# Eight slots instead of four in the row-normalising stage of a graph network

## The reference

```python
h = jnp.maximum(_layernorm(x, axis=-1), 0.0)
x = x + _L0_gnn_ref(h, edge_index, edge_weight, ...)

def _bn(x, g, b):
    m = jnp.mean(x, axis=0)
    v = jnp.var(x, axis=0)
    return g * (x - m) * jax.lax.rsqrt(v + EPS) + b
```

## Time and profile before

| what | value |
|---|---|
| median of three runs | 4132.0 us |
| the profiled execution | 4137.27 us, span 4135.5 us |
| mean granted TensorE clock | 0.869 |
| TensorE, VectorE, ScalarE, GpSimd busy | 75%, 59%, 45%, 35% of the span |
| HBM traffic | 664 MB read, 528 MB written, 288 GB/s over the span |
| the normalising stage | first load 39 us, last GpSimd write issued by 665 us |

### The profile page before, as it was taken

One profiled execution on the slowest core, in us unless ns is written; L12 is line 12 of the kernel. 1 busy time (PEld: TensorE's weight loads), 2 busy tenths in 40 slices (PEclk: granted clock), 3 DMA queues, 4 the chain that ended last, 5 costly groups with the idle time before them and its releaser, 6 DMA issues. The chain is left out here.

```text
span 4135.5 us, 50004 instructions
## 1 busy us (share of the span) xinstructions
PE 3115.6 (75%) x11465; PEld 1891.5 (46%) x11465; DVE 2439.3 (59%) x5239; ACT 1850.5 (45%) x3090; POOL 1430.2 (35%) x1395
## 2 busy tenths in 40 slices
PE   2444443888888883999999999995999999844543
PEld 2444443444444441655655655553444444333432
DVE  4444443777777774888888888783444444433332
ACT  2544452666566661444444444442334444333332
POOL 0332334455555533333333333312222222024344
PEclk8767766999999996999999999997999999955555
DMA  4555553778787775999999999985999999799997
GB/s 129 169 163 179 165 164 117 240 277 282 274 283 283 282 276 171 319 331 346 326 341 340 321 334 336 328 307 184 357 354 353 354 358 354 286 381 380 416 374 308
DMA packets 387808, 1193.34 MB, mean 289 GB/s; under 512 B 61095, under 2 KB 133912, under 8 KB 337570
## 3 DMA queue, kind: packets, MB, share of 16 engines
q1 hardware_dynamic: 282816, 998.32, 65.9%
q0 software_dynamic: 47040, 90.56, 8.9%
q10 hardware_dynamic: 57890, 103.80, 6.6%
HBM read 664.34 MB, written 528.12 MB: 288 GB/s over the span
## 5 line engine op out<-in xcount | busy, mean ns | idle before, releaser
L1000 ACT ACTIVATE l_dn_ho<-l_ps,bias_fold 128x512 f32<-128x512 f32 x588 | 399.2, 687 | 470.0 <-PE l_ps L988 436.3
L1116 POOL DMA_INDIRECT l_ed_gathered<-agg_rows,pos_cols x392 | 403.8, 1030 | 564.0 <-PE l_ps L1151 446.9
L589 PE MATMUL norm_ln_ps<-norm_ln_ho 128*128 128x130 f32 x1568 | 294.4, 372 | 325.3 <-ACT norm_ln_ho L577 324.4
L577 ACT ACTIVATE norm_ln_ho<-norm_ln_x,norm_ln_nbias,norm_ln_rstd 128x128 f32<-128x128 f32 x784 | 306.7, 479 | 294.2 <-DVE norm_ln_nbias L530 256.4
L589 PEld LDWEIGHTS norm_ln_ps<-norm_ln_ho 128*128 128x128 f32 x1568 | 285.0, 284 | 334.9 <-ACT norm_ln_ho L577 333.7
L1123 POOL DMA_INDIRECT l_ed_x_rows<-in_x,dst_cols x196 | 195.5, 997 | 670.6 <-DMA x_dst<-l_ed_x_rows 625.1
L1011 DVE BATCH_NORM_STATS2 bn_stats_all<-l_dn_ho 128x512 f32 (+1 forms) x588 | 370.6, 678 | 80.3 <-ACT l_dn_ho L1000 75.5
L674 PE MATMUL l_ps<-l_dn_columns,w_fold 128*128 128x512 f32 x784 | 379.6, 609 | 47.8 <-ACT l_dn_ho L697 31.8
L988 PE MATMUL l_ps<-l_dn_top,wroot_top 128*128 128x512 f32 x784 | 334.6, 427 | 68.0 <-ACT l_dn_ho L1000 68.0
L503 DVE BATCH_NORM_STATS2 norm_ln_bs<-norm_ln_x 128x6 f32<-128x128 f32 x784 | 192.2, 282 | 297.1 <-DMA norm_ln_x<-in_x 293.5
L697 ACT ACTIVATE l_dn_ho<-l_ps,bias_fold 128x512 f32<-128x512 f32 x392 | 265.1, 687 | 204.9 <-PE l_ps L674 133.7
(11 more groups left out here) (195 smaller groups left out, 5432.0 us busy)
## 6 DMA issues: line engine op xcount, KB each, us to landing
h_dense<-l_dn_ho SPq DMA_DIRECT2D x196, 1024.0 KB, 15.6
l_dn_hi<-h_dense SPq DMA_DIRECT2D x196, 1024.0 KB, 13.5
l_dn_rows<-h_rows SPq DMA_DIRECT2D x98, 520.0 KB
h_rows<-norm_ln_ho SPq DMA_DIRECT2D x97, 520.0 KB, 4.9
l_ed_hd<-h_dst SPq DMA_DIRECT2D x98, 512.0 KB
h_dense<-l_dn_ho SPq DMA_DIRECT2D x98, 512.0 KB, 7.3
out_od_hi<-h_dense SPq DMA_DIRECT2D x98, 512.0 KB
norm_ln_x<-in_x SPq DMA_DIRECT2D x97, 512.0 KB, 4.2
```

The lines of the kernel that those rows point to most:

```text
L577: ins = act.activation(ho[:, j, g, 0:C], xt[:, j, g, :], ACT.Relu, bias=nb[:, j, g:g + 1], scale=rs[:, j, g:g + 1])
L589: ins = pe.matmul(ps[:, 0, 0:TC], ho[0:rows, j, g, 0:C], ho[0:rows, j, g, :], start=first and g == 0, stop=final and g == G - 1, skip_grou ...
L1000: act.activation(ho[:, j, m, c * CW:(c + 1) * CW], ps[:, u % 2, 0:CW], ACT.Relu, bias=bf[:, m:m + 1]).then_inc(rl[j], 1)
L1116: pool.indirect_dma_start(tg[:, j, g, :], None, tab[n - 1][:, :], bass.IndirectOffsetOnAxis(ap=pos_c[:, t:t + 1], axis=0)).then_inc(gat[j] ...
```

## The change

The stage gets a slot count of its own, `LS` = 8, for all its buffers, semaphores and loops; a round is eight tiles and there are 13 rounds (`LI`). Stores stand six tiles behind loads instead of four. `pipeline`, `side_by_side` and `uses` take the number of tiles from the caller, since 13 rounds of eight exceed it by more. The setup makes a second table, `rounds_norm`, in which a round is eight tiles, and the scatter's gate reads that one: it waits for slots 0 and 1 by the first entry and for slots 2 to 7 by the second. The last stage keeps `rounds_first`. The two buffers of the stage double in size.

```diff
+LS = 8
...
-                    if not isinstance(at, int) or at >= 0 and at * slots + slot < units(slots):
+                    if not isinstance(at, int) or at >= 0 and at * slots + slot < (total or units(slots)):
...
+    LI = -(-NT // LS)
...
-                link(dve.tensor_copy(rounds_first[:, :, :], count[:, :, :]))
+                link(dve.tensor_copy(rounds_first[:, :, :], count[:, 0:2, :]))
+                link(dve.tensor_reduce(count[:, 2, :], above[:, :, 1::2], AXIS.X, ALU.add))
+                link(dve.tensor_scalar(count[:, 3, :], count[:, 2, :], float(LI - 2), None, ALU.min))
+                link(dve.tensor_copy(rounds_norm[:, :, :], count[:, 2:4, :]))
...
-            got, mom, nrm, hn = (ph.slots(f"ln_{n}", NS) for n in ("rows", "moments", "scales", "normalised"))
-            step, summed = ph.slots("ln_step", NS), ph.slots("ln_summed", NS)
+            got, mom, nrm, hn = (ph.slots(f"ln_{n}", LS) for n in ("rows", "moments", "scales", "normalised"))
+            step, summed = ph.slots("ln_step", LS), ph.slots("ln_summed", LS)
...
-            xt, ho = ph.sb("ln_x", [P, NS, G, C]), ph.sb("ln_ho", [P, NS, G, TC])
+            xt, ho = ph.sb("ln_x", [P, LS, G, C]), ph.sb("ln_ho", [P, LS, G, TC])
...
-                return NS, [(0, load), (4, store)], end
+                return LS, [(0, load), (6, store)], end
...
-        def gated(pool, stored, g, per):
-            firsts = [pool.value_load(rounds_first[0:1, r, g:g + 1], min_val=0, max_val=DI - 1 - r) for r in range(2)]
-            for r, first in enumerate(firsts):
-                for s in stored[r * NS // 2:(r + 1) * NS // 2]:
+        def gated(pool, table, rounds, stored, g, per):
+            firsts = [pool.value_load(table[0:1, r, g:g + 1], min_val=0, max_val=rounds - 1 - r) for r in range(2)]
+            for first, slots in zip(firsts, (stored[:2], stored[2:])):
+                for s in slots:
                     pool.wait_ge(s, first * per + per)
...
-                            gated(pool, stored, t // (ES * EG), 16)
+                            gated(pool, rounds_norm, LI, stored, t // (ES * EG), 16)
...
-            stored = ph.slots("ln_stored", NS)
-            side_by_side(ph, DI, [norm_rows(ph, stored), map_scatter(ph, stored)])
+            stored = ph.slots("ln_stored", LS)
+            side_by_side(ph, LI, [norm_rows(ph, stored), map_scatter(ph, stored)], NT)
```

More of the change, by code:

```diff
@@ L102, in wait_use, with pipeline @@
     eng.wait_ge(sem, i * per + (base + (per if upto is None else upto)))
-def pipeline(eng, rounds, streams):
+def pipeline(eng, rounds, streams, total=None):
     streams = [x for x in streams if x[1]]
@@ L134, in pipeline, with uses, side_by_side @@
         round_(i)
-def uses(slots, j):
-    return len(range(j, units(slots), slots))
-def side_by_side(ph, rounds, works):
+def uses(slots, j, total=None):
+    return len(range(j, total or units(slots), slots))
+def side_by_side(ph, rounds, works, total=None):
     block = ph.start()
@@ L149, in run @@
         if parts:
-            pipeline(eng, rounds, [(slots, stages) for slots, stages, _ in parts])
+            pipeline(eng, rounds, [(slots, stages) for slots, stages, _ in parts], total)
             for _, _, end in parts:
@@ L193, in build @@
     assert (N, E) == (NODES, EDGES) and E == PS * TS and ET == TB * TR and FULL + PL * G == N and NT * ES == EC * NS
+    assert NT % NS == NT % LS == 2 and LS == 2 * NS
     H1 = prm["W1"].shape[1]
@@ L292, in build @@
             last_node, last_f = ph.sb("last_node", [1, EI], I32), ph.sb("last_node_f", [1, EI])
-            above, count = ph.sb("above", [1, EI, DI - 1]), ph.sb("rounds", [1, 2, EI])
+            above, count = ph.sb("above", [1, EI, DI - 1]), ph.sb("rounds", [1, 4, EI])
             pst, pst2, pst3, pst4 = ph.pb("ps", 1), ph.pb("ps2", 1), ph.pb("ps3", 1), ph.pb("ps4", 5)
@@ L486, in store @@
                     wait_use(sp, hn[j], i)
-                    k = i * NS + j
+                    k = i * LS + j
                     sp.dma_start(tile_of(h0, k), ho[0:held(k), j, :, :]).then_inc(stored[j], 16)
                 def end():
-                    for j in range(NS):
-                        sp.wait_ge(stored[j], 16 * uses(NS, j))
-                return NS, [(0, load), (4, store)], end
+                    for j in range(LS):
+                        sp.wait_ge(stored[j], 16 * uses(LS, j, NT))
+                return LS, [(0, load), (6, store)], end
             def vector(dve):
@@ L562, in end @@
                 def end():
-                    dve.wait_ge(summed[(NT - 1) % NS], uses(NS, (NT - 1) % NS))
+                    dve.wait_ge(summed[(NT - 1) % LS], uses(LS, (NT - 1) % LS, NT))
                     dve.tensor_copy(moments[:, :], ps[:, 0, 0:TC]).then_inc(kept, 1)
                     dve.wait_ge(kept, 1)
-                return NS, [(0, first_moments), (2, scales)], end
+                return LS, [(0, first_moments), (2, scales)], end
             def scalar(act):
@@ L621, in end @@
                     pool.wait_ge(sem, 16 * ET)
-                return NS, [], end
+                return LS, [], end
             return dict(gpsimd=gpsimd)
```

17 lines of the change are left out of this document (9 added, 8 removed).

## The result

The changed kernel takes 3986.55 us (median of four runs, 3979.04 to 3996.41); the kernel before, on the same chip, 4131.82 (four runs, 4129.2 to 4133.24). The ratio is 0.9651, with a 95% interval from 0.9628 to 0.9673: faster by 145 us, where 264 were forecast, and above the forecast's range (3845 to 3905). The profiled execution took 3996.41 us, its span is 3994.6, its mean granted clock 0.889.

The account below looks back on a forecast made before the run. Bound: a latency ring of loads, VectorE and ScalarE in the normalising stage, no engine. Saved 275.3, less 10.2 for the tail and 1.3 for clears, gives 263.8: 4132.0 to 3868 us, range 3845 to 3905.

Parts of the forecast that it names:

- The ring opens: Normalising stage: with eight slots the load, VectorE, ScalarE cycle of 12.26 us a pair falls to 2.5 us a tile.
- The pace, 6.4 us a pair: Normalising stage: ScalarE at 6.26 and DMA at 6.2 nearly tie, so 49 pairs at 6.4 take 313.6 us.
- Loop passes, 7 us: Normalising stage: ScalarE loses 0.7 us at each of 10 passes of eight tiles.
- VectorE's "1.4 us" for each pass: Normalising stage: VectorE stands still about 1.4 us once in most loop passes, hidden behind ScalarE.
- Three irregular stalls: ScalarE in the normalising stage: 32.0 us idle, about 15 beyond the usual; 5 us taken as remaining.
- The tail, +10.2 us: GpSimd's scatter behind the normalising stage's last tile: eight more writes wait, growing it from 12.2 to about 22.4 us.
- the clears of semaphores: Behind the normalising stage: 28 more semaphores to clear cost 0 to 3.9 us, 1.3 taken.
- the stretch: Normalising stage, first pair to end of last: 325.6 us against 600.9, so 275.3 saved.
- DMA did not bound: Rival, normalising stage: DMA engines are the bound at 6.9 us a pair, kernel 3893 us; chance 0.17.
- TensorE's granted clock: Rival, normalising stage: TensorE stays at 1.2 GHz, 7.2 us a pair, kernel 3908 us; chance 0.05.
- the lead was gained: Opposite rival: SyncE's ordered queue keeps loads late, pairs stay at 12.26 us, kernel 4143.5 us; chance 0.02.
- Every round of eight pays a fetch stall: Rival, normalising stage: 13 rounds stall 5.6 us extra each, 73 us against 12, kernel 3929 us; chance 0.05.

Follow-up runs that it names:

- coarse4: The kernel before, with its four slots and loops, only the map scatter's gate made to count rounds of eight tiles; 4239.09 us, ratio 1.0122 on chip 6.
- fine_gate: The changed kernel with its eight slots, but the scatter's gate counting rounds of four tiles as before; 4000.09 us, ratio 0.9543 on chip 6.
- after_again: The changed kernel, unaltered, run again on chip 7; 3826.05 us, ratio 0.9398 to the kernel before on that chip.

## Why the prediction was wrong, step by step

- **The ring opens**: right. VectorE's wait for rows went from 264 to 3 us, SyncE's load line waits no more.
- **The pace, 6.4 us a pair**: a little high. Where nothing stalls it is 301.73 / 49 = 6.16, within 0.01 on all three chips, ScalarE's own pace without a seam. DMA, with 2.11 MB in 6.16 us (343 GB/s by that count, 335 in the window's row, which holds the end of the loads), was nearly tied, as said, but overlapped.
- **Loop passes, 7 us**: no cost at all; one row of 784 activations has no pause. VectorE's "1.4 us" for each pass was misread: it is what a run of eight writes does, as the pass without writes at 402.7 us and the kernel before on chip 7 show. The rule of the Trainium skill weighed there (Runtime: NRT & Kernel Launch, section "Instruction fetch mechanics") says that a taken branch to code outside the two blocks held makes the engine wait for a fetch. No run here shows such a cost: in the stage of the changed kernel the instruction queues carry 14 packets for ten passes, and writing the rounds out changes nothing: the stage is 301.7 to 301.8 us either way on the chips without stalls, and on chip 2 the pauses are there without loops.
- **"Three irregular stalls ... the lead will eat part, none may be left: I take 5 us"**: this is the term that failed. ScalarE's idle time, for which it and the 7 us of loop passes were the forecast, measured 122 us. The three stalls were taken for noise of fixed number that a lead in tiles would absorb. They belong to GpSimd's long runs of writes. The gate that opens every eight tiles makes more of these (coarse4 shows that part by itself: on the old ring 51 us, 41 of them besides the tail), and the shorter stage crowds the same 196 writes (fine_gate, 107.6 us idle with the gate as fine as before). The ring of before, in which ScalarE waits some 5.6 us for each pair anyway, hid part of it: a run of sixteen cost it 4 to 6 us net in the kernel before, where ScalarE at its own pace loses 10 to 12. In hindsight, with the eight runs of 16 and 24 writes that the change showed, priced at 1.27 us for each write beyond the eighth (the three stalls of the earlier trace rows are 10 to 11 us), 6 x 10.2 + 2 x 20.4 = 102 us would have stood in the place of the 5: 3868 + 97 = 3965, beyond the range and within 22 us of the result. The prediction itself had the run lengths in hand ("16 issues take 20.4 us") and used them only to show that GpSimd would keep up.
- **The tail, +10.2 us**: right. The last write is issued by 499.12 + 0.91 = 500.0, 22.5 us behind ScalarE's end; 22.4 were forecast. The gap grew by 12.6, so up to 2.4 us are left for the clears of semaphores, where 1.3 was taken.
- **The books**: the stretch came out 426.1 - 325.6 = 100.5 us over, the gap 12.6 - 11.5 = 1.1, the next stage 26.4, the others -5.0: 123 us, and 3873.5 + 123 = 3996.5 is the profiled execution's 3996.41.
- **Not forecast at all**: 26.4 us given back in the next stage. 12 of them lie before the end of its first pass; of the other passes two take 40.6 us where 35 is usual (before, one takes 38.3). There too GpSimd runs gathers while the others work, but that these are the same stalls was not tested; 8 to 12 us of the 26 also stand on the chips without stalls.

On the chips without stalls the change saved 4073.29 - 3826.05 = 247, 239 and 250 us, where 264 were forecast. The stretch came down by 273.7 us on chip 7, where 275.3 was the term; that the two agree is in part luck, since it began at 575.4 us and not at 600.9, and ended at 301.7 and not at 325.6.

Of the rivals, none happened. DMA did not bound; TensorE's granted clock was 1.00 where it was fed (0.76 in the stalled window, in which it was busy 22.5 of 50 us), which is also what the Trainium skill says in TensorE: Matmul & The Clock Gate, section "What's actually happening", of sustained work; the lead was gained. The rival "Every round of eight pays a fetch stall" (3929, chance 0.05) has the right place, the crossing of a round, and the right stall, 11.1 us, but the wrong mechanism: it was tied to a fetch. Its price was 5.6 us a round, the usual wait of the old ring taken off, where six runs cost about 10.5 each and two about 22.

Left open: why some chips stall (the chip of the result, 6 and 2) and others not (7, 13, 14), whether ordinary writes of GpSimd would do it too, what sets the loss apart from the length of a run, and what the engines lack in a stalled stretch. That their instructions come late fits TensorE's single passes and the register instructions at 0.70 us, but no record names what they wait for.

## What to carry to other kernels

Before pricing irregular stalls as noise, lay their times beside what every other engine does then, the ones off the critical path too; if they go with something, ask how often the change makes it happen. A wait that is taken away no longer hides what else was late: the ring of before absorbed part of each stall. A coarser gate does not only delay work, it bunches it, and a bunch of GpSimd's indirect writes can cost the others more than the delay itself (coarse4: 41 us against 10). A gain that rests on one chip's trace should be timed on a second: here the same two kernels differ by 3.5% on one and 6% on another.

## What the hardware showed that was not expected

- On the chip of the result and on chips 6 and 2, beside long runs of indirect writes from GpSimd (1.27 us each), TensorE got one pass each 2.8 us, SyncE's register instructions took 0.70 us, VectorE started nothing for up to 7.67 us, and ScalarE, at its own pace otherwise, lost about 10 us for sixteen writes and 22 for 24. On chips 7, 13 and 14 83 writes in a row (from 270.1 to 374.6 us on chip 7) did not slow the stage.
- On the chip of the result a run of eight cost a pair of tiles about 1 us in the kernel before, with a pause of VectorE of some 1 us that looks like a cost of the loop; it is absent where nothing is written (389 to 427 us) and on chip 7.
- The kernel before takes from 4071 to 4188 us on different chips, 2.9% apart, with its executions on chip 7 within 0.24% (4068 to 4077.6).
- Loads and stores mixed ran at 335 GB/s at a DMA share of 0.96 for 250 us (after_again, 100 to 350), with ScalarE never late.
